# Moving all four heads' probabilities through memory in a fused attention and mixture-of-experts kernel

## The reference

```python
q = (layernorm(x) @ w_q)          # 16 heads of 64
k, v = context @ w_k, context @ w_v
attn = softmax(einsum('bhid,bhjd->bhij', q, k) * 64 ** -0.5)
x = x + einsum('bhij,bhjd->bhid', attn, v).reshape(B, S, 1024) @ w_o + b_o
...
x = x + experts(layernorm(x))     # top 2 of 8, capacity 640, exact gelu
```

## Time and profile before

| | us |
|---|---|
| median of 3 runs | 930.26 (929.24 to 930.47) |
| profiled execution, time | 926.51 |
| profiled execution, span from first to last instruction | 924.8 |
| TensorE busy in the span | 893.8 (97%) |
| VectorE busy | 721.4 (78%) |
| ScalarE busy | 539.3 (58%) |
| GpSimd busy | 401.9 (43%) |
| squares<-prob, 56 issues of 768 KB, median to landing | 5.7 |
| probt<-squares, 224 issues of 192 KB, median to landing | 3.9 (SP), 4.0 (ScalarE's queue) |

### The profile page before, as it was taken

How to read it: one execution, slowest core, us unless ns; L and a number is a source line. 1 busy time by engine, 2 the same in 40 slices (tenths; PEclk the granted TensorE clock), 3 DMA queues, 4 the chain that set the end, 5 groups by cost and what they waited for, 6 DMA issues and landing times.

```text
span 924.8 us, 21960 instructions
## 1 busy us (share of the span) xinstructions
PE 893.8 (97%) x7692; PEld 792.9 (86%) x7692; DVE 721.4 (78%) x1601; ACT 539.3 (58%) x1544; POOL 401.9 (43%) x597
## 2 busy tenths in 40 slices
PE   7999999999999999999999999999889999999995
PEld 7878888888888888888888888888689999999995
DVE  5757778888797788889888887888887877668762
ACT  5887765666666576676667667656643443334420
POOL 5561424545463553636455363633543222332223
PEclk9999999999999999999999999999999999999998
DMA  8464677668777767766766777667148557554322
GB/s 236 147 206 121 210 218 218 198 204 234 219 217 221 221 187 214 230 202 213 241 191 183 219 227 206 196 211 226 44 136 179 91 135 150 122 129 64 107 30 29
DMA packets 152989, 162.61 MB, mean 176 GB/s; under 512 B 62140, under 2 KB 141610, under 8 KB 152752
## 3 DMA queue, kind: packets, MB, share of 16 engines
q1 hardware_dynamic: 127920, 130.21, 48.1%
q10 hardware_dynamic: 16128, 22.03, 8.6%
q0 software_dynamic: 8832, 8.98, 5.6%
HBM read 96.83 MB, written 69.29 MB: 180 GB/s over the span
## 4 chain that ended last, share of the span: by engine, by line
PE 58%; DVE 15%; DMA 10%; ACT 8%; issue 4%; SPq 4%; POOL 0%; POOLq 0%; ACTq 0%; DVEq 0%
PE psum L802 15%; PE psum L1070 10%; PE psum L1054 10%; DMA squares<-prob 8%; PE psum L929 7%; PE psum L913 7%; PE psum L869 5%; ACT prob L1142 3%; DVE negmax L1335 2%; DVE prob L1364 2%; PE psum L892 2%; DVE hidl L1281 2%; SPq L516 2%; DVE bufl L1281 1%; DVE ql L1324 1%
## 5 line engine op out<-in xcount | busy, mean ns | idle before, releaser
L1142 ACT ACTIVATE prob<-psum,negmax 128x256 f32<-128x256 f32 x512 | 240.8, 492 | 137.1 <-DVE negmax L1335 137.1
L1335 DVE TENSOR_REDUCE negmax<-psum 128x2 f32<-128x512 f32 x256 | 158.5, 681 | 30.5 <-PE psum L869 30.5
L663 POOL TENSOR_TENSOR al<-attended,ah 128x512 fp32r<-128x512 f32 x56 | 72.4, 1293 | 196.4 <-ACT ah L1081 196.3
L778 POOL DMA_INDIRECT out_rows<-y,rowi x40 | 66.1, 1652 | 159.2 <-DVE y L1592 152.3
L1253 ACT ACTIVATE hid<-psum,b1t 128x640 f32<-128x640 f32 x64 | 50.9, 796 | 126.7 <-PE psum L1054 126.7
L913 PE MATMUL psum<-probt,v 128*64 128x256 f32 x1024 | 124.6, 385 | 0.0
L1142 ACT ACTIVATION_READ_ACCUMULATOR prob<-psum,negmax 128x1 f32 x512 | 114.6, 224 | 0.0
L1364 DVE STREAM_TRANSPOSE prob<-prob 128x1024 f32<-128x1024 f32 x112 | 107.9, 963 | 0.0
L913 PEld LDWEIGHTS psum<-probt,v 128*64 128x64 f32 x1024 | 67.7, 136 | 38.4 <-issue 9.7
L733 POOL DMA_INDIRECT slot_table<-row,picki x64 | 66.5, 1039 | 62.0 <-PE psum L802 25.7
L1070 PE MATMUL psum<-w2h,hidh 128*128 128x256 f32 x320 | 91.2, 285 | 1.4 <-DVE hidl L1281 1.4
(11 more groups left out here) (209 smaller groups left out, 2625.6 us busy)
## 6 DMA issues: line engine op xcount, KB each, us to landing
squares<-prob SPq DMA_DIRECT2D x56, 768.0 KB, 5.7
probt<-squares SPq DMA_DIRECT2D x112, 192.0 KB, 3.9
probt<-squares ACTq DMA_DIRECT2D x112, 192.0 KB, 4.0
invrows<-inverses SPq DMA_DIRECT2D x128, 128.0 KB, 3.6
w1r<-in_w SPq DMA_DIRECT2D x8, 1024.0 KB, 5.3
w2r<-in_w SPq DMA_DIRECT2D x8, 1024.0 KB, 9.3
slot_table<-blank SPq DMA_DIRECT2D x8, 662.5 KB, 6.5
blocks<-slot_table SPq DMA_DIRECT2D x56, 80.0 KB, 2.5
```

The lines of the kernel that those rows point to most:

```text
L663: pool.tensor_tensor(al[:, b % 2, c:c + 2, :], attended[:, :, :], ah[:, b % 2, c:c + 2, :].bitcast(F32), ALU.subtract).then_inc(sem("a_lo" ...
L778: pool.indirect_dma_start(out=out_rows, out_offset=bass.IndirectOffsetOnAxis(ap=rowi[:, e % 2, s:s + 1], axis=0), in_=y[:, e % 2, s, :], i ...
L1142: last = act.activation(into, out_of, ACT.Exp, bias=negmax[:, m % 2, u, qb:qb + 1], accum_out=total[:, m % 2, u, qb:qb + 1])
L1335: dve.tensor_reduce(negmax[:, m % 2, u, :], psum[:, u, :].rearrange("p (q s) -> p q s", q=ST), AX.X, ALU.max, negate=True).then_inc(sem("m ...
```

## The change

All four heads of the periods in MOVED now go through memory: HEADS is 4, and `by_pe` gives TensorE none of them. `turn3` and `copy3` of these periods are gone. The second part of `square` takes heads 2 and 3. The store is of 1024 KB, and each of the four reads is of 256 KB. On TensorE `v(m)` comes ahead of `pv(m - 2)`. On ScalarE `v_sb(m)` comes first, then `move_high(m - 1)` and `a_hi(m - 2)` in odd periods, `a_hi(m - 2)` and `move_high(m - 1)` in even ones. On SP `move_low(m - 1)` comes behind `inv_in(m - 1)` instead of behind `inv_out(m - 1)`. The reciprocals are laid down in another order of heads, so that `inv_in` reads each half's inverse sums as one whole row of 2 KB.

```diff
--- before.py
+++ after.py
@@ -63,7 +63,7 @@
 
 
 MOVED = range(6, PERIODS - 2)
-HEADS = 3
+HEADS = UNITS
 
 POOL_REST = range(PER_B, PERIODS - 4)
 SQ = 32
@@ -72,7 +72,7 @@
 
 def by_pe(m):
 
-    return (HEADS,) if m in MOVED else (0, 1, 2, 3)
+    return () if m in MOVED else (0, 1, 2, 3)
 
 
 def turns_to(m, u):
@@ -108,7 +108,7 @@
             out += [("q", m + 1), ("turn0", m - 1), ("k", m + 1), ("turn1", m - 1), ("v", m), ("turn2", m - 1)]
         else:
             out += [("scores", m)] + ([("logits", b - 3)] if r == 0 and 3 <= b else [])
-            out += [("q", m + 1), ("k", m + 1), ("turn3", m - 1), ("pv", m - 2), ("v", m)]
+            out += [("q", m + 1), ("k", m + 1), ("v", m), ("pv", m - 2)]
         if r == (1 if b else 2) and b + 1 < B:
             out += [("xt", b + 1)]
         if r == 2 and 1 <= b:
@@ -126,8 +126,9 @@
             out += [("copy0", m - 1), ("exp2", m), ("k_hi", m + 1), ("copy1", m - 1), ("exp3", m), ("copy2", m - 1),
                     ("v_sb", m)]
         else:
-            out += [*steps("exp0 exp1", m), ("q_hi", m + 1), ("exp2", m), ("k_hi", m + 1), ("exp3", m),
-                    ("move_high", m - 1), ("copy3", m - 1), ("a_hi", m - 2), ("v_sb", m)]
+            out += [*steps("exp0 exp1", m), ("q_hi", m + 1), ("exp2", m), ("k_hi", m + 1), ("exp3", m)]
+            out += [("v_sb", m), ("move_high", m - 1)] if m % 2 else [("v_sb", m)]
+            out += [("a_hi", m - 2)] + ([] if m % 2 else [("move_high", m - 1)])
         if r == (1 if b else 2) and b + 1 < B:
             out += [("xt_hi", b + 1)]
         out += [("copy3", m - 1)] if four else []
@@ -175,22 +176,22 @@
 
 
         out += [("load_ctx", 2)] if m == 2 else []
-        out += [("inv_out", m - 1)] + ([("move_low", m - 1)] if m - 1 in MOVED else [])
+        out += [("inv_out", m - 1)]
         out += [("traffic", b - 2)] if r == 1 and 2 <= b else []
-        out += [("inv_in", m - 1)] + ([("lift", m)] if m in MOVED else [])
+        out += [("inv_in", m - 1)] + ([("move_low", m - 1)] if m - 1 in MOVED else []) + ([("lift", m)] if m in MOVED else [])
         out += [("load_ctx", b + 2)] if r == 3 and 1 <= b < B - 2 else []
         out += {2: steps("clear", 0), 3: steps("clear", 1), 4: steps("clear", 2)}.get(m, [])
 
 
     c, d, e, m, z = B - 3, B - 2, B - 1, PERIODS - 2, PERIODS - 1
     o0, o1 = ST * e, ST * e + 1
-    out += [("scores", m), ("q", z), ("k", z), ("turn3", m - 1), ("pv", m - 2), ("v", m),
+    out += [("scores", m), ("q", z), ("k", z), ("v", m), ("pv", m - 2),
             ("o", ST * d), ("x2t", c), ("scores", z), ("pv", m - 1), ("logits", c),
             *steps("turn0 turn1 turn2 turn3", m), ("v", z), ("o", ST * d + 1), ("pos", c), *steps("turn0 turn1", z),
             ("pv", m), *steps("turn2 turn3", z), ("o_most", o0), ("x2t", d), ("pv", z), ("logits", d), ("o_most", o1),
             ("o", o0), ("o", o1), ("pos", d), ("x2t_part", o0), ("x2t_part", o1), ("logits_part", o0),
             ("logits_part", o1), ("spread", 0), ("spread", 1), ("pos", e), ("base", 0), ("spread", 2), ("spread", 3)]
-    out += [*steps("exp0 exp1", m), ("q_hi", z), ("exp2", m), ("k_hi", z), ("exp3", m), ("move_high", m - 1), ("copy3", m - 1), ("a_hi", m - 2), ("v_sb", m), ("x2t_sb", c), ("w_hi", 0), ("w_hi", 1),
+    out += [*steps("exp0 exp1", m), ("q_hi", z), ("exp2", m), ("k_hi", z), ("exp3", m), ("v_sb", m), ("move_high", m - 1), ("a_hi", m - 2), ("x2t_sb", c), ("w_hi", 0), ("w_hi", 1),
             *steps("exp0 exp1", z), ("a_hi", m - 1), ("copy0", m), ("exp2", z), ("copy1", m),
             ("exp3", z), *steps("copy2 copy3", m), ("gate_exp", c), ("v_sb", z), ("w_hi", 2), *steps("copy0 copy1", z),
             ("w_hi", 3), ("a_hi", m), *steps("copy2 copy3", z), ("x2t_sb", d), ("row_hi", d), ("a_hi", z),
@@ -206,7 +207,7 @@
             ("x2add", o1), ("stat", o1), ("center", o0), ("center", o1), *steps("slot high onehot carry", d),
             *steps("bias compare rank", e), *steps("gate keys", d), *steps("row_lo slot high onehot shift", e),
             ("pick", d)]
-    out += [*steps("inv_out move_low inv_in", m - 1), ("load_w", 0), *steps("inv_out inv_in", m), ("inv_out", z),
+    out += [*steps("inv_out inv_in move_low", m - 1), ("load_w", 0), *steps("inv_out inv_in", m), ("inv_out", z),
             ("traffic", d), ("inv_in", z), ("load_base", 0), ("traffic", e), ("load_w", 1)]
     out += [("iota", 0), ("scatter", c - 1), ("w_lo", 0), ("w_lo", 1), ("ln2_root", d), ("scatter", c),
             ("ln2_root", e), ("scatter", d), ("scatter", e)]
@@ -513,8 +514,8 @@
                 if m >= 2:
                     sp.wait_ge(sem("a_norm"), m - 1)
                 for h in range(2):
-                    sp.dma_start(invrows[h * HD:(h + 1) * HD, m % 2, :, :],
-                                 inv_table[m % 2][0:UNITS * ST].rearrange("(c h q) p -> h c (q p)", h=2, q=ST)[h]
+                    sp.dma_start(invrows[h * HD:(h + 1) * HD, m % 2, :, :].rearrange("p c s -> p (c s)"),
+                                 inv_table[m % 2][0:UNITS * ST].rearrange("(h x) p -> h (x p)", h=2)[h]
                                  .partition_broadcast(HD))\
                       .then_inc(sem(f"inv_in{m % 2}"), 16)
 
@@ -1341,8 +1342,8 @@
                     dve.wait_ge(sem("inv_clear"), 1)
                 if m >= 2:
                     dve.wait_ge(sem("inv_out"), 16 * (m - 1))
-                dve.reciprocal(invtot[:, m % 2, 0:UNITS * ST], total[:, m % 2, :, :].rearrange("p u q -> p (u q)"))\
-                   .then_inc(sem("inv_total"), 1)
+                dve.reciprocal(invtot[:, m % 2, 0:UNITS * ST].rearrange("p (h c q) -> p h c q", h=2, c=2),
+                               total[:, m % 2, :, :].rearrange("p (c h) q -> p h c q", h=2)).then_inc(sem("inv_total"), 1)
                 dve.wait_ge(sem("inv_total"), m + 1)
                 dve.transpose(invturned[:, m % 2, :], invtot[:, m % 2, :]).then_inc(sem("inv"), 1)
 
@@ -1357,7 +1358,7 @@
 
             def square(m, part):
 
-                heads = (slice(0, 2), slice(2, HEADS))[part]
+                heads = slice(2 * part, 2 * part + 2)
                 dve.wait_ge(sem("exp"), UNITS * m + heads.stop)
                 c = ST * S // GROUPS
                 at = prob_most(m).rearrange("p (g c) -> p g c", g=GROUPS)[:, :, heads.start * c:heads.stop * c]
```

## The result

The changed kernel takes **1007.73 us** (median of four runs, 1005.34 to 1009.06); the kernel before, measured beside it, takes 930.37 (929.24 to 930.68). The ratio is 1.0833, 95% interval [1.082, 1.0846]: 77.4 us slower, where the prediction had 911 and a range that ended at 930. The profiled execution took 1005.34 us, its span is 1003.6.

What follows compares the result with a forecast made beforehand. TensorE, busy 97% of the span, was taken as the bound: 29.7 us off its list, less 7.8 at the logits and 2.6 for late reads, gives 19.3 us gained and 911 us against the 930.26 median; range 903 to 930.

Steps and rivals of the forecast that it cites:

- From 1.7 us early to 1.2 late: SP's read-backs against r=2's value products (r: period number modulo 4); priced at 0.2 us per batch, 2.6 us in all.
- The queue falls to 0.49 in r=3, so lateness doesn't pile up: Argument against late reads stalling every batch: the DMA engines' busy share drops to 0.49 in r=3.
- 6.8 us of room, the same case: ScalarE's half of the reads, behind attended in even periods: 6.8 us left before the value products, like SP's half.
- TensorE's 0.53 us per period: Head 3's four transposes leave TensorE: 0.53 us in each of 56 periods, 29.7 us at most.
- The logits' 0.93 us: TensorE's idle time before the logits grows from 0.33 to 0.93 us per batch, giving back 7.8 us.
- the 0.55 us of VectorE: Second block transpose takes two heads instead of one: 0.55 us more per period, with room left on VectorE.
- The span of the forecast: Stalls of 0 and 1.2 us at either end give 904 to 917, a few microseconds taken in for r=3's chain.
- DMA work of 35.7 us per batch: DMA engines' work rises from 29.1 by 6.6 us to 35.7 of some 38.7 us per batch, 92%.
- the inverse rows at 0: Rows of inverse sums read in pieces of 2 KB instead of 1 KB, same bytes: 0, perhaps a few tenths gained.
- the pitch as a small matter: Memory rows go from 6144 to 8192 B apart, a power of two; by the Trainium skill this costs nothing.
- The slower one: Rival, DMA ring as bound: SP's queue empty some 2 us per period until the inverse sums land; 950 us, chance 0.12.
- Reads land late: Rival: each batch stalls 1.2 us or more at r=2's value products; 6.3 us gained, 924 us, chance 0.22.

Runs made afterwards that it cites:

- e10: Changed kernel with SP's reads ahead of the inverse rows, ScalarE's behind v's copy, VectorE transposing four heads, the fourth neither stored nor read back; 934.93 us.
- e12: Changed kernel with SP's reads put back ahead of the inverse rows and ScalarE's reads behind the copy of v in every period; 968.65 us.
- e4: Kernel before without head 3's transposes on TensorE and their copy on ScalarE in MOVED, nothing put in their place; 912.78 us.
- e18: e10 with VectorE's two layer norm instructions moved behind the next entry's statistics; 919.02 us, ratio to before 0.9875.
- e2: Changed kernel with ScalarE's reads behind the copy of v in every period, SP's order as changed; 1001.04 us.
- e1: Changed kernel with only SP's reads put back ahead of the wait for the inverse sums; 969.68 us.
- e7: Kernel before with only the change's whole rows of inverse sums; 928.41 us, ratio to before 0.9995.
- e6: Changed kernel with each row of the square table padded by 512 B, rows 8704 B apart instead of 8192; 995.56 us.
- e5: Changed kernel with the 1 MB store of squares issued from ScalarE's queue, behind attended's copy, instead of from SP's; 1024.19 us.

## Why the prediction was wrong

The loss adds up: before 930.0, e10 934.9 (+5.0), e12 968.7 (+33.7, the last quarter of the bytes), changed kernel 1007.7 (+39.1, the two orders). The kernel before beside e10 took 928.3, so the first step may be 6.7. It is e4's -17.2 and then +22.2 from e4 to e10, which differ in VectorE's extra work and in the places of the value products and of ScalarE's copies. The trace puts nearly all of it down to the logits: 16.6 us of waits for 9.4, and nine slow stretches of some 1.5 us.

- **"From 1.7 us early to 1.2 late", 0.2 us per batch for late reads: the step that failed.** The idle time in the changed kernel is 5.7 us per batch, and in the batch shown the first read-back lets the products go 3.2 us late. Three terms were too small. The small write ahead of the reads was given a landing of about 2 us and took 4.31 in the chain, because the 1 MB store stands ahead of it in SP's queue. The reads were given the median of before plus 1 us, 5.2; they took 6.36 and 8.93. And the store's own landing went from 5.7 to 7.3 and more (e12), with SP's half of the reads ahead of it in the queue and ScalarE's beside it.
- **"The queue falls to 0.49 in r=3, so lateness doesn't pile up": false.** The share is of bytes, not of the loop. Store, landing, reads, next store is one chain on SP that had 4 us of slack per batch at least and has none at 1 MB (e12). The new order puts VectorE's inverse sums and a third landing into each round, which no share shows.
- **ScalarE's half, "6.8 us of room, the same case": false.** attended waits for the value products and the read-back for attended, so a late product makes a late read. It is worth 6.7 us (e2) while the products are late, and nothing otherwise (e12 against e1).
- **TensorE's 0.53 us per period: too large.** It measured 0.44 (e4). That the start-to-start of the transposes holds a changeover which stays with the value products would explain it, but isn't shown.
- **The logits' 0.93 us: right for the chain it followed (0.91 in e18), too small for the kernel (1.28 in e10).** The sum had priced the 0.55 us of VectorE as free outside r=3. In e10 attended comes later in r=2, and with it GpSimd's instruction lies beside the layer norm's (e18).
- **Missing altogether: the clock.** Some of the stalls of 1.3 to 3.2 us brought the lower level, others (2.11 us in e12) didn't. In twelve batches TensorE is busy for 39.50 us per batch where e4 has 38.13: 1.4 us per batch.
- **The span of the forecast: a slip.** By the sum itself a stall of 0 and of 1.2 us gives 908 and 924, not 904 and 917; the range of 903 to 930 holds both.
- **Right:** DMA work of 35.7 us per batch (0.82 x 45.24 = 37.1), the second transpose at 1.23 us, the inverse rows at 0 (e7), the pitch as a small matter (e6).
- **The rivals.** The slower one, 12% at 950, had SP's gap at the small write and too small a price: it let ScalarE's reads fill the gap and counted no wait of the products. Its thought that the small write stands behind the store in its ring is what the packets show. "Reads land late" had the place right and a fifth of the size.

## What to carry to other kernels

For data that go out to memory and come back, add up one round of the loop (store, landing, reads, landing, and whatever the issuing queue waits for in between) with landings as they are under the load that the change makes, and compare it with the period; a share of busy DMA engines does not bound it. Before a wait is put behind a small write, count what stands ahead of that write in its own queue. Price a stall of TensorE with the slow matmuls that may follow it. When VectorE's work moves by half a microsecond, look at what GpSimd's then lies beside, and look for a copy that the stalled engine needs behind one that is still waiting: moving it ahead gave 0.6% here.

## What the hardware showed that was not expected

- A stall of 1.28 us ahead of the logits was followed by 3.4 us of matmuls at half speed in e10 (375.4 to 378.7, about 1.5 us lost); one as long at 334.3 was not, nor was one of 2.11 us in e12. The length of the stall alone doesn't decide it.
- The 16 KB store of inverse sums took 4.3 us to land behind 1 MB in its own queue and kept SP waiting for up to 7.2 us; 3.0 us with its queue empty and the 1 MB on the other (e5), 2.0 with both nearly empty.
- ScalarE's queue read 22.03 MB back at 277 GB/s before (8.6% of 924.8 us); the changed kernel's 29.37 MB came at 234 (12.5% of 1003.6), e12's at 301 (10.1% of 966.9).
- A layer norm instruction of VectorE goes from 0.41 to 1.22 us beside GpSimd's subtraction of two tiles (e10).
